# First attention: the scores by key moved behind the values in TensorE's order

## The reference, cut to what matters

```
q = (x @ wq).reshape(Bq, Tq, N_KV, N_REP, HEAD_DIM)        # 16 batches, 256 tokens, 2 x 4 heads
k_lat = (x @ wk_down).reshape(Bq, Tq, N_KV, D_LAT)         # 32 wide
k = jnp.einsum('bkhl,ld->bkhd', k_lat, wk_up)
scores = jnp.einsum('bqhrd,bkhd->bhrqk', q, k) * scale
scores = jnp.where(causal, scores, jnp.finfo(scores.dtype).min)
probs = jax.nn.softmax(scores, axis=-1)
y = jnp.einsum('bhrqk,bkhd->bqhrd', probs, v)
return y.reshape(Bq, Tq, N_HEADS * HEAD_DIM) @ wo
```

## Time and profile before

| | us |
|---|---|
| median of 3 runs | 1805.56 |
| lowest, highest | 1804.36, 1808.79 |
| the profiled execution | 1806.83 |
| its span, first to last instruction | 1805.0 |

### The profile page before, as it was taken

The page is one execution under the profiler, slowest core; times in us unless marked ns, Lnnn a source line. Parts: engine busy times, 40 slices in busy tenths (PEclk is TensorE's granted clock), DMA queues, the critical chain, the costliest instruction groups (busy, mean ns, idle before and its releaser), DMA issues.

```text
span 1805.0 us, 34492 instructions
## 1 busy us (share of the span) xinstructions
PE 1217.3 (67%) x11544; PEld 898.8 (50%) x11545; DVE 1134.6 (63%) x2883; ACT 786.3 (44%) x1164; POOL 969.0 (54%) x1052
## 2 busy tenths in 40 slices
PE   2298578786297126999945388787875236999871
PEld 2198456564297102899822144443442213999730
DVE  6546657676446882334576699898997872334642
ACT  2154256673153011454411288788886111555310
POOL 0624335452524177756666266676764077747675
PEclk9998689996598558999978555555555568999986
DMA  9133124420132011666421000000000012656423
GB/s 360 61 92 105 46 92 153 153 92 2 63 92 68 12 43 53 204 190 192 152 53 47 13 2 2 3 1 2 1 1 1 1 48 83 193 185 192 141 53 83
DMA packets 99999, 150.43 MB, mean 83 GB/s; under 512 B 21408, under 2 KB 54816, under 8 KB 99104
## 3 DMA queue, kind: packets, MB, share of 16 engines
q1 hardware_dynamic: 58656, 75.30, 12.9%
q0 software_dynamic: 20480, 41.98, 8.0%
q10 hardware_dynamic: 20736, 31.47, 5.4%
HBM read 74.16 MB, written 74.45 MB: 82 GB/s over the span
## 4 chain that ended last, share of the span: by engine, by line
PE 43%; DVE 19%; POOL 13%; issue 11%; SPq 5%; DMA 4%; ACT 2%; DVEq 0%; ACTq 0%; POOLq 0%
POOL slots_top L624 9%; PE PS L906 9%; PE PS L845 5%; PE PS L928 5%; POOL AREA L1086 4%; SPq L1285 3%; DVE X L1107 3%; PE PS L298 3%; PE PS L299 3%; PE PS L300 3%; PE PS L891 2%; PE PS L914 2%; PE PS L1729 2%; DVE AREA L1895 2%; PE PS L1745 2%
## 5 line engine op out<-in xcount | busy, mean ns | idle before, releaser
L624 POOL DMA_INDIRECT slots_top<-XN,ROW x320 | 317.3, 992 | 289.6 <-DVE ROW L578 183.5
L1086 POOL DMA_INDIRECT AREA<-results_top,ROW x320 | 305.7, 955 | 241.0 <-DMA results_top<-AREA 122.1
L998 DVE SCALAR_TENSOR_TENSOR AREA<-PS,AREA 128x512 f32<-128x512 f32 x96 | 66.4, 692 | 220.0 <-ACT AREA L975 219.5
L1690 POOL TENSOR_TENSOR AREA<-AREA 128x1024 f16<-128x1024 f32 x64 | 151.3, 2364 | 92.3 <-ACT AREA L1830 92.1
L906 PE MATMUL PS<-WGU,AREA 128*128 x768 | 185.7, 385 | 0.0
L1919 DVE TENSOR_REDUCE AREA<-PS 128x4 f32<-128x1024 f32 x128 | 156.1, 1219 | 30.4 <-PE PS L1717 29.6
L1823 ACT ACTIVATE AREA<-PS,AREA 128x1024 f32<-128x1024 f32 x128 | 142.7, 1115 | 53.0 <-PE PS L1729 52.8
L906 PEld LDWEIGHTS PS<-WGU,AREA 128*128 128x128 f32 x768 | 141.2, 194 | 16.2 <-ACT AREA L965 0.2
L1318 POOL TENSOR_TENSOR AREA<-AREA 128x1536 f16<-128x1536 f32 x32 | 92.9, 2902 | 99.4 <-ACT AREA L1533 99.4
L417 PE MATMUL PS<-IDF,XN 128*128 128x128 f32 x192 | 49.7, 417 | 134.3 <-DVE XN L407 134.3
L1830 ACT ACTIVATE AREA<-AREA 128x1024 f16<-128x1024 f32 x128 | 135.5, 1059 | 0.0
(11 more groups left out here) (260 smaller groups left out, 3548.1 us busy)
## 6 DMA issues: line engine op xcount, KB each, us to landing
AREA<-slots_top SPq DMA_DIRECT2D x96, 256.0 KB
results_top<-AREA ACTq DMA_DIRECT2D x96, 256.0 KB
slots_top<-ZERO SPq DMA_DIRECT2D x24, 512.0 KB, 3.1
AREA<-slots_top SPq DMA_DIRECT2D x48, 128.0 KB
results_top<-AREA ACTq DMA_DIRECT2D x48, 128.0 KB
AREA<-query_rows SPq DMA_DIRECT2D x48, 128.0 KB, 2.9
slots_top<-XN,ROW POOLq DMA_INDIRECT x320, 2.2
AREA<-results_top,ROW POOLq DMA_INDIRECT x320
```

The source lines that it names most:

```text
L624: nc.gpsimd.indirect_dma_start(out=L.xs[q], out_offset=bass.IndirectOffsetOnAxis(ap=ROW[:, n:n + 1], axis=0), in_=XN[:, t * D:(t + 1) * D] ...
L1086: nc.gpsimd.indirect_dma_start(out=slots[L.tag][u][:, c * D:(c + 1) * D], out_offset=None, in_=L.ys[g * GT // L.tiles], in_offset=bass.Ind ...
L1690: nc.gpsimd.tensor_tensor(PB1[1][:, g, :], PF1[:, g, :], PB1[0][:, g, :], ALU.subtract).then_inc(b_plo[1].sem, 1)
```

## The change

In TensorE's loop over slots, by_key of t is written after values of t-2 and before values_turned of t-3. Before, it stood after max_turned of t+1 and before project of t-4. Nothing else is altered.

```
--- before.py
+++ after.py
@@ -1491,14 +1491,14 @@
                     upper(t + 2)
                 if exists(t + 1):
                     max_turned(t + 1)
-                if exists(t):
-                    by_key(t)
                 if exists(t - 4):
                     project(t - 4, sent)
                 if exists(t + 2):
                     lower(t + 2)
                 if exists(t - 2):
                     values(t - 2)
+                if exists(t):
+                    by_key(t)
                 if exists(t - 3):
                     values_turned(t - 3)
```

## The result

The changed kernel takes 1866.8 us (median of 4 runs, 1864.83 to 1870.19) against 1806.44 us of the kernel before in the same comparison. The ratio is 1.033, with a 95% interval of 1.031 to 1.036: 60 us slower, where 49 was forecast.

A forecast was written before the change was run, and what follows sets the result against it. SyncE's queue, 10.89 us for two units, was taken as the bound. Rings +39.5 and clock +9.6 make 49.1 us on the median 1805.56: 1854.7, given as 1855; 8 in 10 for 1838 to 1874.

The forecast's parts named there:

- The bound before: First attention: SyncE's issues of maxima, zeros and query rows take 10.89 us for two units and set the pace.
- The rings: First attention: two loops of waits back to the scores by key, now closing once a slot; +39.5 us together.
- the first ring: Plain (even) slots: scores by key, exponential, p_hi, values_hi, values_lo, values, next scores by key; 6.04 us a slot.
- the other: Odd slots, with a query batch: exponential, p_hi, query copy, q_lo, max_upper, lower, values, scores by key; 8.09 us.
- the pieces' own time: TensorE's project, lower and values, put ahead of the scores by key: their time counts for nothing, filling the wait.
- The clock: TensorE in odd slots: half the granted clock after an idle stretch, in 8 of 13 slots; +9.6 us.
- The price of one: One clock fall on TensorE: 1.04 us for scores by key, 0.2 for lower and values together; 1.2 a slot.
- my sign for 8 cases: Profile of the changed kernel: odd slots showing scores by key of 2.3 us in about 8 cases confirm the clock's part.
- The wait of project: TensorE's project waiting for q_lo in odd slots; the forecast's ring counted no such wait, going over max_upper and lower.
- The clock that stays down: Rival: TensorE's clock stays low and every slot of the attention pays, 39 us; 1884 us, chance 0.14.
- The gain: Rival: values and lower find inputs ready, so TensorE's 28.3 us wait at L1443 becomes work; 1777 us, chance 0.05.
- the no change: Rival: SyncE's 10.89 us for two units stay the bound and the move is hidden; chance 0.05.

The follow-up runs named there:

- e8: Kernel before, with SyncE's reads of the query rows put behind the rows of the maxima; 2296.5 against 2307.4 us, ratio 0.994.
- e1: Kernel before, with the scores by key put behind project alone, ahead of lower and values; 1804.0 us, ratio 0.9995.
- e12: Kernel before, with values put ahead of the scores by key, project still first and lower last; 2370.1 us against 2307.4, ratio 1.027.
- e5: Changed kernel, with ScalarE's p_hi done one slot later, behind the copy of the maxima and ahead of the next exponential; 1816.5 us, ratio 1.007.
- e3: Changed kernel, with VectorE's max_upper put ahead of q_lo in odd slots; 1847.7 us, ratio 1.024.

## Why the prediction was right

**The bound before.** SyncE's queue, with 10.89 us for two units, was named from the earlier trace rows, as issues; some 1.2 us of it was the wait for the landing. e8, which takes this wait out and moves the maxima ahead of the reads, bears the queue out: 10.9 us of the whole went, and 14.9 of the stage (172.2 to 157.3), where the waits for the landing had been 18.3. Of a stage read from one execution a few us are chance; e1, which is no faster, has 167.7.

**The rings.** The step that carried the forecast, that values_lo and max_upper are late next, was right in place and size: 8.09 and 6.04 forecast, 8.10 and 6.12 measured. e12 shows that the first ring needs the values alone, e5 that p_hi is in it, e3 that q_lo is in the other. The forecast for the stage at the full clock was 211.7; with the clock held it was 214.2. For the rings 39.5 us were forecast and 42.0 came. The forecast took the pieces' own time for nothing and still had the 0.90 of values and 0.45 of lower in both sums; the sums are right, since work that closes a ring counts in it.

**The clock.** This is the term that was mis-sized, 9.6 us against 16.7. The count was wrong: I took 8 of 13 odd slots; slot 1 was slowed, 11 of the 12 from 3 to 25, and four of the last five slots, for which I had taken none. The 11 lost 12.2 us together and the four 4.2. The price of one was near, 1.1 and not 1.2, but in part by luck. I had 1.04 for the scores by key and 0.2 for lower and values together. In slot 13 the scores by key took 1.95 instead of 1.27, lower 0.82 instead of 0.45, and values 1.08 instead of 0.90, which makes 1.23. Scores by key of 2.2 to 2.3 us, my sign for 8 cases, are in seven of these odd slots; in four others the clock fell sooner and rose before they ended. The idle stretch was 2.69 us, shorter than my "some 3 us", and ahead of project, not of lower, since project waits for q_lo. Falls came after it all the same. My measure, one idle stretch of 3.68 with a fall and one of 2.08 without, said little about how often: ten of the eleven stretches of 2.69 were followed by a fall and one was not. Of the 60.4 us measured against 49.1, the clock makes 7.1, the rings 2.5, and 1.7 lie outside the stage.

**The wait of project** for q_lo (29.6 us in 11 waits) stood in the code, and I left it out of the ring. It did not matter, since max_upper ends 1.2 us later than q_lo.

**The rivals.** The clock that stays down (1884) did not come: it rose again in each plain slot up to 28. The gain (1777) and the no change are refuted by the time, and the steps say why. The maxima's transfers had slack, as forecast: L1443 waits for no DMA any more.

## What to carry to other kernels

Before moving a piece in an in-order stream behind another, list what the other waits for, and follow each wait back until it reaches the piece itself. If it does, count the slots that the way round now has: here the way stayed the same, 6.1 and 8.1 us, but it closed in one slot instead of two. The wait that an engine shows (28.3 us at L1443) is no gain to be had if what would be put there has a later release. And a piece that waits may still be worth its place early, if an engine behind it is in order: project cost TensorE 29.6 us of waiting, and putting it last cost 19 us more, about 6 by the engine behind it and the rest by half the clock.

## What was not expected of the hardware

An idle stretch of TensorE of 2.69 us every 15 us was followed by half the granted clock in ten of eleven slots, and 15 matmuls of 512 columns without use per two slots held it at 1.00 for the 140 us looked at. More work made the stage shorter, by 16.7 us. What makes the one stretch of 2.69 us differ from the other ten stays open. The same attention stage ran step for step alike (8.10 and 6.12) on a chip on which the whole program took 28% longer, 2307 instead of 1804 us, with much longer waits in its expert layers; steps within a stage could be compared across chips, times and ratios could not.
